# Weights of an attention kernel loaded from the inputs in quarters instead of through a DRAM copy, and values by one transfer

## The reference

```python
q = hidden_state @ Wq + bq
k = encoder_hidden_state @ Wk + bk
v = encoder_hidden_state @ Wv + bv
scores = jnp.einsum('bkgld,bksd->bkgls', q, k) * scale
scores = scores + encoder_attention_mask[:, :, None, :, :]
attn = jax.nn.softmax(scores, axis=-1)
out = jnp.einsum('bkgls,bksd->bkgld', attn, v)
out = out.transpose(0, 3, 1, 2, 4).reshape(b, l, H)
out = out @ Wo + bo
x = out + hidden_state
return (x - mu) * jax.lax.rsqrt(var + EPS) * gamma + beta
```

## Time and profile before

| | us |
|---|---|
| median of 3 runs | 1751.57 |
| lowest and highest | 1750.95 and 1754.67 |
| the profiled execution, its own time | 1751.32 |
| its span, first to last instruction | 1749.3 |
| TensorE busy | 1602.6 |
| VectorE busy | 1448.7 |
| ScalarE busy | 1385.7 |
| GpSimd busy | 935.7 |

### The profile page before, as it was taken

How to read it: one execution, slowest core, us unless ns; L and a number is a source line. 1 busy time by engine, 2 the same in 40 slices (tenths; PEclk the granted TensorE clock), 3 DMA queues, 4 the chain that set the end, 5 groups by cost and what they waited for, 6 DMA issues and landing times. The chain is left out here.

```text
span 1749.3 us, 38438 instructions
## 1 busy us (share of the span) xinstructions
PE 1602.6 (92%) x14048; PEld 1110.0 (63%) x14048; DVE 1448.7 (83%) x2773; ACT 1385.7 (79%) x3186; POOL 935.7 (53%) x731
## 2 busy tenths in 40 slices
PE   3898879999899989999899998999989999999986
PEld 2665556576566765676576775667666676667654
DVE  4489878789788996889888898789988899788886
ACT  3578868769888787978889789787888878887794
POOL 5426433526754458534675448662585545856382
PEclk8999999999999999999999999999999999999998
DMA  9669987646885578664796567965678646875331
GB/s 178 186 148 227 241 232 199 182 135 168 250 257 144 138 187 286 188 154 122 209 288 185 130 175 192 287 178 127 174 238 252 158 133 170 292 208 150 84 114 67
DMA packets 357292, 325.02 MB, mean 186 GB/s; under 512 B 145776, under 2 KB 248176, under 8 KB 357104
## 3 DMA queue, kind: packets, MB, share of 16 engines
q1 hardware_dynamic: 357104, 322.56, 67.5%
HBM read 244.85 MB, written 83.89 MB: 188 GB/s over the span
## 5 line engine op out<-in xcount | busy, mean ns | idle before, releaser
L1941 PE MATMUL bank<-ring_hi,w_sb 128*128 128x512 f32 x2368 | 785.5, 399 | 32.1 <-issue 19.2
L1725 ACT ACTIVATE probs<-probs,shift 128x512 f32<-128x512 f32 x1024 | 726.9, 713 | 92.1 <-DVE shift L1826 91.0
L1839 DVE STREAM_TRANSPOSE turned_p<-probs 128x2048 f32<-128x2048 f32 x256 | 585.7, 2297 | 154.3 <-PE bank L2021 149.3
L1826 DVE CUSTOM_DVE_ANT_0 probs<-bank,mask_l 128x512 f32<-128x512 f32 x1024 | 643.1, 680 | 56.3 <-PE bank L2001 37.2
L1626 POOL TENSOR_TENSOR w_sb<-w_raw,w_sb 128x512 fp32r<-128x512 f32 x320 | 412.1, 1297 | 413.8 <-ACT w_sb L1682 413.7
L1941 PEld LDWEIGHTS bank<-ring_hi,w_sb 128*128 128x128 f32 x2368 | 444.4, 189 | 149.9 <-issue 42.6
L1941 PE MATMUL bank<-ring_lo,w_sb 128*128 128x512 f32 x1184 | 467.9, 395 | 0.0
L2001 PE MATMUL bank<-k_stack,q_stack 96*128 96x512 f32 x1024 | 358.9, 414 | 12.7 <-DVE shift L1826 10.0
L2021 PE MATMUL bank<-turned_p,v_all 32*32 32x512 f32 x8192 | 307.9, 642 | 65.8 <-DVE turned_p L1839 48.6
L1638 POOL TENSOR_TENSOR ring_lo<-x_t,ring_hi 128x512 fp32r<-128x512 f32 x168 | 214.7, 1291 | 144.9 <-ACT ring_hi L1694 144.4
L2001 PEld LDWEIGHTS bank<-k_stack,q_stack 96*128 96x128 f32 x1024 | 186.1, 189 | 143.3 <-issue 62.9
(11 more groups left out here) (75 smaller groups left out, 933.2 us busy)
## 6 DMA issues: line engine op xcount, KB each, us to landing
w_raw<-w_d SPq DMA_DIRECT2D x144, 256.0 KB, 3.7
q_stack<-q_hi_d SPq DMA_DIRECT2D x128, 256.0 KB, 4.3
w_raw<-in_L_xattn_Wo_dram SPq DMA_DIRECT2D x128, 256.0 KB, 3.0
q_hi_d<-part_hi SPq DMA_DIRECT2D x64, 256.0 KB, 3.9
q_lo_d<-part SPq DMA_DIRECT2D x64, 256.0 KB, 5.0
q_stack<-q_lo_d SPq DMA_DIRECT2D x64, 256.0 KB, 3.9
v_all<-v_d SPq DMA_DIRECT2D x256, 64.0 KB, 2.2
out_dram<-y_sb SPq DMA_DIRECT2D x32, 512.0 KB, 3.0
```

The costliest lines, as they stand in the source:

```text
L1725: nc.scalar.activation(probs[:, st % 2, h, :], probs[:, st % 2, h, :], ACT.Exp, scale=-1.0, bias=shift[:, g % 2, i:i + 1], accum_out=sums[ ...
L1826: nc.vector.tensor_tensor_reduce(out=probs[:, st % 2, h, :], in0=S_ps[h][:, :], in1=mask_l[:, st, :], scale=-1.0, scalar=HIGHEST, op0=ALU. ...
L1839: nc.vector.transpose(turned_p[:, :, :, st, :].rearrange("p j h c -> p h j c"), probs[:, st % 2, :, :].rearrange("p h (j c) -> p h j c", c ...
L1941: mm = nc.tensor.matmul(C[c][:, :], w_sb[:, n_w, (1, 0, 0)[third], d % 4, :], (hi, lo, hi)[third], start=(n == 0), stop=(n == 23))
```

## The change

Every half of Wq, Wk and Wv is loaded straight from the input in four quarters, as the first ones were. `w_d`, `relay`, the semaphore `relay_in` and the list of places `"relay"` are gone. `load_v` issues one transfer whose source repeats the 32 rows four times. gamma and beta, which were loaded ahead of the first `relay`, are loaded ahead of the first `o_store`. The places of the steps from batch 0 on are new, and with them the order on every engine; the places of the prologue stay but for one store (53.7 to 55.5). The hunks on the tables are cut to a few lines here.

```diff
-BASE = {1: 256.32, 2: 463.56, 3: 671.62, 4: 879.00, 5: 1086.39, 6: 1293.78, 7: 1501.17}
+BASE = {1: 248.76, 2: 453.06, 3: 660.59, 4: 868.21, 5: 1075.84, 6: 1283.46, 7: 1491.09}
...
-        "relay": (162.1, 163.9, 191.35, 204.74, 211.37, 246.36, 263.34, 266.06, 292.85, 302.4, 312.18, 348.22),
...
-        "z_store e": (218.22, 223.74, 228.52, 229.88),
+        "z_store e": (218.35, 223.87, 228.65, 230.01),
...
-    for i, place in enumerate(PLACES["first"]["relay"]):
-        entries.append((place, len(entries), (0, "relay", i)))
...
-        def direct(t, what):
-            return t <= 0 or t == 1 and what == "q"
...
-                    w_count[n % NW] += 64 if direct(t, what) and what != "o" else 16
+                    w_count[n % NW] += 64 if what != "o" else 16
...
-            def relay(i):
-                to = w_d[i].rearrange("p (k c) -> p k c", k=KD)
-                for r, rows in enumerate(rows_of(i)):
-                    sp.dma_start(to[32 * r:32 * (r + 1), :, :], rows).then_inc(relay_in, 16)
...
-                if t == 1:
-                    sp.wait_ge(relay_in, 768)
-                sp.dma_start(to.rearrange("p k c -> p (k c)"), w_d[i][:, 512 * half:512 * (half + 1)])\
-                  .then_inc(w_in[n % NW], 16)
+                w, at = (wk, i) if i < 2 else (wv, i - 2) if i < 4 else (wq, i - 4)
+                rows = w.rearrange("(r k p) c -> r p k c", r=4, p=32)[:, :, 4 * half:4 * (half + 1), at * P:(at + 1) * P]
+                for r in range(4):
+                    sp.dma_start(to[32 * r:32 * (r + 1), :, :], rows[r]).then_inc(w_in[n % NW], 16)
...
-                for r in range(4):
-                    sp.dma_start(v_all[32 * r:32 * (r + 1), g % 2, :],
-                                 v_d[2 * t + g // 4][HD * (g % 4):HD * (g % 4 + 1), :]).then_inc(v_in[g % 2], 16)
+                rows = v_d[2 * t + g // 4][HD * (g % 4):HD * (g % 4 + 1), :]
+                sp.dma_start(v_all[:, g % 2, :], rows.rearrange("(o p) c -> o p c", o=1).broadcast_to([4, HD, NJ * HD]))\
+                  .then_inc(v_in[g % 2], 16)
...
-                if kind == "relay" and e[1] == 0:
+                if n == ROWS_AT:
...
-                        pe.wait_ge(v_in[g % 2], 64 * (4 * t + g // 2 + 1))
+                        pe.wait_ge(v_in[g % 2], 16 * (4 * t + g // 2 + 1))
```

More of the change, by code:

```diff
@@ L180 @@
             (123.82, 126.07),
-            (130.57, 140.28),
-            (144.03, 147.75),
-            (153.6, 167.5),
+            (128.77, 139.62),
+            (143.14, 149.57),
+            (154.52, 166.74),
         ),
         "w_hi kv": (
[L186 to L189, removed]
+            (135.69, 137),
+            (142.24, 150.89),
+            (151.51, 158.53),
+            (166.63, 174.77),
         ),
         "w_lo kv": (
[L192 to L195, removed]
-        ),
[4 rows of a table removed]
+            (136.43, 137.74),
+            (143.05, 151.63),
+            (152.92, 159.27),
+            (167.37, 175.51),
+        ),
[4 rows of a table added]
         "mm q": (
@@ L213 @@
             (45.52, 48.3),
[L214 to L217, removed]
+            (53.7, 55.95),
+            (57.75, 60.43),
+            (65.1, 68.35),
+            (72.54, 92.04),
             (95.29, 99.32),
-            (102.76, 115.19),
+            (103, 115.19),
         ),
@@ L223 @@
             (50.98, 52.7),
[L224 to L227, removed]
+            (60.01, 63.46),
+            (66.77, 71.53),
+            (73.46, 76.84),
+            (77.46, 97.39),
             (101.71, 104.49),
@@ L356 @@
-        "rbc_out": (36.35, 61.66, 95.15, 120.54, 145.36, 170.94, 201.2, 226.78),
-        "norm": (41.04, 63.59, 95.87, 123.15, 151.46, 179.05, 204.05, 228.01),
-        "o_store": (42.75, 65.28, 97.62, 124.84, 153.15, 181.12, 205.74, 229.83),
-        "mask": (-25.15, -18.33, -8.17, -2.77),
[11 rows of a table removed]
+            (27.37, 27.89, 28.41, 28.93),
+            (52.8, 53.32, 53.84, 54.36),
+            (80.49, 81.01, 81.53, 82.05),
+            (108.98, 109.5, 110.02, 110.54),
+            (130.5, 131.65, 132.17, 132.69),
@@ L371 @@
+        "sel": (35.21, 55.29, 83.04, 111.47, 133.69, 161.43, 188.73, 216.46),
+        "rbc": (36.53, 65.65, 90.62, 116.03, 141.05, 166.7, 197.26, 221.72),
+        "rbc_out": (37.55, 66.73, 91.85, 117.03, 141.9, 168, 198.31, 223.31),
+        "norm": (39.81, 68.24, 92.75, 121.93, 143.36, 175.81, 201.11, 226.15),
+        "o_store": (41.58, 69.93, 94.77, 124.07, 146.55, 177.88, 202.88, 229.02),
+        "mask": (-20.5, -15.87, -9.33, -4.27),
[11 rows of a table added]
         "mm kv": (
[4 rows of a table removed]
[4 rows of a table added]
         ),
         "w_load kv": (
-            (107.36, 117.69),
@@ L379 @@
-            (124.15, 125.29),
-            (129.17, 140.33),
-            (143.58, 148.15),
+            (104.05, 114.47),
+            (120.47, 122.27),
+            (125.96, 136.47),
+            (140.19, 144.75),
         ),
         "w_hi kv": (
-            (114.65, 125.84),
-            (129.31, 133.27),
-            (137.29, 144.74),
-            (149.35, 155.17),
+            (111.06, 121.07),
+            (125.86, 133.21),
+            (133.83, 141.28),
+            (145.26, 151.58),
         ),
@@ L423 @@
             None,
-            (-17.96, -15.91),
-            (-8.28, 4.31),
-            (13.07, 25.43),
-            (29.4, 32.17),
+            (-24.98, -16.05),
+            (-15.43, -0.44),
+            (3.56, 18.48),
+            (22.22, 26.12),
         ),
@@ L471 @@
+            (188.58, 189.87),
+            (196.06, 202.23),
+        ),
[4 rows of a table added]
         "mm o": (
[8 rows of a table removed]
[8 rows of a table added]
         ),
         "w_load o": (
-            (22.19, 31.49),
-            (34.51, 43.65),
-            (44.1, 59.14),
-            (67.04, 70.32),
-            (73.1, 76.58),
-            (79.15, 89.81),
-            (93.7, 98.07),
-            (100.59, 103.87),
+            (21.69, 32.02),
+            (35.74, 41.13),
+            (44.29, 58.29),
+            (61.54, 66.1),
+            (68.74, 71.85),
+            (75.34, 86.51),
+            (89.76, 94.32),
+            (97.29, 100.57),
@@ L490 @@
         ),
         "w_hi o": (
-            (35.73, 43.14),
-            (47.14, 52.78),
-            (56.8, 68.05),
-            (74.44, 75.06),
-            (77.36, 82.17),
-            (83.18, 93.84),
-            (100.49, 108.64),
-            (110.64, 114.03),
+            (26.75, 36.93),
+            (42.17, 47.58),
+            (52.18, 62.49),
+            (66.11, 71.27),
+            (75.8, 78.49),
+            (82.57, 90.54),
+            (94.52, 99.49),
+            (101.54, 108.36),
@@ L515 @@
-        "y_add o": (68.88, 74.67, 97, 100.24, 102.22, 122.47, 128.44, 147.58),
+            (28.15, 38.34),
+            (43.55, 48.78),
+            (53.59, 63.23),
+            (67.52, 72.61),
+            (76.54, 79.23),
+            (83.31, 91.28),
+            (95.26, 100.54),
+            (102.28, 109.1),
+        ),
+        "keep o": (61.81, 67.33, 75.12, 88.98, 96.51, 103.54, 120.39, 125.18),
+        "v_turn": (None, None, 155.33, 175.08),
+        "v_store": (None, None, 157.06, 178.33),
@@ L525 @@
-        "z_store o": (171.78, 182.02, 192.52, 200),
-        "root o": 152.47,
-        "rstd o": 162.54,
+            (97.62, 98.27, 99.8, 100.45),
+            (144.73, 145.58, 146.43, 147.28),
+        ),
+        "res o": (-68.59, -68.14, -67.69, -66.79),
+        "aggr o": (145.38, 146.23, 147.08, 147.93),
+        "z o": (161.66, 163.51, 169.28, 177.85),
+        "zmul o": (162.94, 170.42, 179.19, 191.16),
+        "zadd o": (165.39, 175.45, 186.13, 193.61),
+        "z_store o": (168.84, 179.23, 189.58, 198.83),
@@ L528 @@
+        "root o": 148.25,
+        "rstd o": 158.96,
     },
@@ new lines @@
+        "recip": (27.5, 51.82, 70.94, 110.86, 134.9, 160.38, 183.71, 203.27),
+        "spread": (27.82, 52.14, 71.26, 111.18, 135.64, 162.21, 184.42, 210.06),
+        "v_load": (-19.31, 11.79, 30.38, 54.3, 83.19, 111.99, 133.16, 162.03),
+        "pv": (25.28, 49.2, 77.58, 106.89, 128.06, 156.93, 183.14, 212.69),
+        "sel": (32.63, 56.85, 88.61, 117.89, 143.04, 164.54, 196.67, 219.62),
+        "rbc": (38.38, 60.71, 89.69, 119.44, 144.12, 167.94, 197.75, 221.17),
+        "rbc_out": (39.1, 61.99, 90.41, 121.44, 146.48, 168.86, 198.84, 221.89),
@@ L651 @@
+            (142.53, 147.82),
+            (152.23, 156.25),
+        ),
[4 rows of a table added]
         "mm q": (
@@ L780 @@
+        "z_store o": (185.42, 192.23, 198.45, 209.97),
+        "root o": 152.81,
+        "rstd o": 177.29,
     },
@@ L1187, in attention_kernel @@
         o_d = dram("o_d", [NB * NG, P, L], F32)
-        w_d = dram("w_d", [12, P, KD * P], F32)
         ident = sb("ident", [P, P], F32)
@@ L1255, in attention_kernel @@
         biases_in, bias_scaled = sem("biases_in"), sem("bias_scaled")
-        relay_in = sem("relay_in")
```

(14 more changed lines are left out.)

813 lines of the change are left out of this document (385 added, 428 removed), and 318 rows, old and new, of the table PLACES.

## The result

Over 20 runs each, the changed kernel takes a median of 1755.56 us (1751.32 to 1760.82) against 1751.24 us (1746.10 to 1759.29) for the kernel before: a ratio of 1.0021, 95% interval 1.0011 to 1.0030. The forecast was 1742 with a range of 1736 to 1752. The change is slower by 0.2%, little but outside the interval of the noise, instead of faster by 0.5%. The profiled execution has a span of 1757.9 us, at the upper end of its runs.

The account below looks back on a forecast made before the run. The prediction saw no single idle resource, with batch 0 crowded at SyncE's queue and the DMA engines. Span 1749.3 - 9.95 + 0.6 = 1739.95, plus 2.02 outside it and 0.25 to the median, gave 1742 us; range 1736 to 1752.

Parts of the forecast that it names:

- Values by one transfer: Loads of values on SyncE's queue: 1.4 less issue time per group, 11 per batch, hidden; effect on the time nothing.
- the rivals, with a chance of 0.09: Values' transfer carried by only four engines delays loads queued behind it; 2.5 us over six batches, 1757 us; chance 0.09.
- Copies gone and new order: SyncE's queue in batch 0 freed of 48 copies, later work moves forward; last place falls by 9.95 us.
- Reading the places as microseconds: Table of places taken as times: trace leaves them by 0.5 us over 829 us between batches 3 and 7.
- Nothing to gain: Rival: batch 0's idle time is lack of work and the copies were hidden; 1751.6 us; chance 0.05.
- Kept, and given back: Rival: batch 0 gains, middle batches wait for weights at their crowded end, 1.5 us each; 1750.6 us; chance 0.13.
- The quarters: Weight halves as four quarters: 0.78 us more of the DMA engines each, middle-batch DMA share from 0.70 to 0.79.
- The loss of 0 to 0.6 us: Waits for quartered weights in batches 1 to 6: taken as 0.1 us a batch, 0.6 in all.
- Batches of 207.6 us: Sign after the change: batches take 207.6 us, the new order's step being 207.62; 209 or more proves it wrong.
- waits of a few us: Sign after the change: ScalarE's waits for loaded weights stay at a few us.
- SyncE's waits between 160 and 270 us: Sign in batch 0: the queue's waiting rises well above 4 us.
- Moving gamma and beta: Two 512 KB loads moved to about 100 us: costs nothing, 2.6 us if not.

Follow-up runs that it names:

- new_v4: Changed kernel with the values of a group loaded by four transfers again, all else as changed: 1740.22 us, ratio 0.9938.
- new_v4_again: The same kernel as new_v4, timed and profiled once more: 1740.99 us, ratio 0.9935.
- old_quarters: Kernel before with all halves of Wq, Wk, Wv direct in quarters and no copies to w_d; old order, four transfers of values: 1750.63 us, ratio 1.0003.
- kind 5: In loads_alone, 256 KB loaded from runs of 512 bytes in one transfer: 2.6 us alone, 9.1 us for eight in a row.
- loads_alone: Separate kernel without attention: SyncE issues five kinds of 256 KB load, alone and eight in a row; eight took 8.3 to 22.9 us.
- new_long_rows: Changed kernel, values still by one transfer, weight halves from batch 1 on replaced by stand-ins of 128 rows of 2 KB: 1745.27 us, ratio 0.9969.
- old_v1: Kernel before with one edit, the values of a group loaded by one transfer: 1756.03 us, ratio 1.0027.

## Why the prediction was wrong

**The step that failed** is "Values by one transfer": "nothing", because the values are loaded 37 us before their use. That is beside the point: the values had time enough, and what suffered was what is queued behind them on the four engines that carry them. The term measured 1755.56 - 1740.22 = 15.3 us. The mechanism stood among the rivals, with a chance of 0.09 and at 15 us. That the size agrees is luck, as its sum had the places and the delays wrong (next paragraph), and left out the granted clock. The chance was too low. I let "no row bears it out" speak against a rule, although no row spoke against it either, and a load whose slowest dimension is 4 was new to this kernel.

**The place of the cost** was wrong in the rival too. It counted only two loads in each middle batch, one being half 1 of output tile 5, with 4.2 us to its use, and a delay of up to 2 us. In the middle batches the waits of 2.58, 2.15 and 1.69 us are for another half, the second of output tile 0 (place 35.89, behind the values at 30.38): its use stands 10 us behind its load, and it lands after 7.6 to 12.9 us, 5 to 9 us later than in `new_v4`. Why it is so much more than the 2.9 us of one transfer of values is not shown. And 7 to 12 us of the 18 to 24 between the profiles arise before batch 1, where 106 of 110 us of SyncE's queue were issuing before and the direct loads follow the values at once.

**Copies gone and new order.** The size held: 9.95 us forecast with 0.6 lost, and `new_v4` is 10.4 us below the kernel before by the medians, 10.9 by the ratio. Its `rbc_out` came at 289, 705 and 1541 us, in `new_v4_again` at 294, 713 and 1547, where 293, 714 to 715 and 1545 were named. The reason was half right. Removing the copies alone gave nothing (`old_quarters`), as the old order could not use the room; the new order with the copies was 10.7 us slower than before. Reading the places as microseconds gave the right size, as it priced both together; why the places come so near to the measured times is not shown. The rival "Nothing to gain" is out for the whole change but describes `old_quarters` exactly. "Kept, and given back" had the crowded end of the batches right as the place of a loss, but not its cause: with four transfers of values the batches from 1 to 7 take 208.6 us on average.

**The quarters.** 0.78 us of the engines for each half was mis-sized; it measured 0.40. The 45 ns for a packet of 512 bytes was read from the first 30 us by putting all of the time down to 5345 packets and none to the 1972 smaller ones, which are not few; kind 5 of `loads_alone` had 28 ns. The DMA share of a middle batch of `new_v4` is 0.73, not 0.79. The loss of 0 to 0.6 us held. What they do is lengthen the delay behind the values in the middle batches, as `new_long_rows` shows; that this is because they fill the same four engines further is the likely reading, not seen engine by engine.

**The rest.** Batches of 207.6 us and waits of a few us were not seen in the changed kernel; without the values' transfer most batches took 208 to 209 us, and the waits for weights were 13.5. SyncE's waits between 160 and 270 us rose as said, to 15.9 in `new_v4`. Moving gamma and beta was not tried apart.

**Left open:** how much of the 15 us is waiting and how much is TensorE's lower clock after it; and a single transfer of values with an outermost dimension of 16 or more, which was not tried.

## What to carry to other kernels

Fewer transfers are not less work for the DMA engines: look at how many engines one transfer gets, by its share and its GB/s while it drains alone, or by its semaphore packets. A load that has all the time in the world can still cost, through what is queued behind it on the same engines. Waits for the load itself don't show it; the landings of unedited loads do, best that of the load right behind it (a half of Wo: 12.5 us instead of 3.6), while a median over all is blunt (`w_d` in `old_v1`: 4.6 instead of 3.7). Keep the four transfers: the kernel `new_v4` beats both.

## What the runs showed of the hardware

One transfer of 128 packets of 2 KB whose source had an outermost dimension of 4 used four engines, 102 GB/s in all, 2.9 us each in a row and 4.9 alone (`loads_alone`); the same bytes from 128 rows ran on 16, 2.5 us alone. Its issue took a median of 532 ns in the changed kernel, against 421 for a transfer of 32 partitions before. A single issue can hold SyncE's queue for long, and not only this one: 3.24 us for the values at 198.76, 3.60 for a quarter of Wk in the same kernel, 2.88 for a quarter of Wq in the kernel before. Packets of 512 bytes, with the engines full, moved 297 GB/s, those of 2 KB 363.
